# A decoder kernel with a new order in its first stage, gate and up projections apart in the experts, and one swap in the last stage

## The chip, the cores and the metric

One core of one Trainium2 chip runs the whole program in one launch. The metric is device time in microseconds (us), from three runs of the kernel before and as many of the kernel after. Engines are called PE (TensorE, the matmuls), PEld (its weight loads), DVE (VectorE), ACT (ScalarE), POOL (GpSimd) and SP (which only issues DMAs here).

## The reference

Two decoder layers on x of 8 x 256 tokens x 512 features, in float32, each sublayer followed by a layer norm of the sum. What matters here:

```python
# layer 0: differential attention, 16 pairs of heads of width 16 (4 shared key pairs), causal
q, k, v = x @ Wq.T, x @ Wk.T, x @ Wv.T
probs = softmax(mask(q k^T / 4)); o = probs @ v
attn = o[even heads] - lambda_full * o[odd heads]
attn = attn * rsqrt(mean(attn**2) + 1e-5) * ln_w * (1 - LAMBDA_INIT)
x = layernorm(x + attn @ Wo.T)
# layer 0: long convolution over pairs of channels with the context, plus a skip term; layernorm
# layer 0: 8 experts, the 2 best of each token
y = (silu(h @ gate.T) * (h @ up.T)) @ down.T      # gate, up: 512 -> 352; down: 352 -> 512
# layer 1: causal attention of 16 heads; attention over context and new tokens;
# layer 1: attention with keys and values picked from one of 16 heads by a gate
idx = argmax(x @ W_gate.T); k_shared = k[head idx]; v_shared = v[head idx] * top gate value
```

## The kernel before, in words

The program is a row of stages with a barrier between them: front (layer 0 attention and the sums of the skip term), conv (long convolution), middle (norms, routing), experts, tail (all of layer 1). In each stage every engine runs its own list of instructions in order; semaphores tie them together. No planner is in it: the order in the source is the order on the engine.

**Front.** One batch of 256 tokens passes through four phases, one a round, so that in round r the batches d = r, a = r-1, f = r-2 and u = r-3 are worked on together (`rounds()`). There are 11 rounds with work (r = 0 to 10); d ends after r = 7, a after r = 8, f after r = 9. On PE, batch d is transposed (`turn`) and projected (`query` x4, `value`, `key`). Batch a gets six score tiles (`score`, four banks of PSUM each), from which DVE takes the row maxima (`maxima`). All six share one tile of PSUM (`quads` has a single entry), so score n+1 waits for maxima n. Then `split_top` and `shift` bring the maxima to PE, six transposed score tiles (`scoreT`) follow, ACT takes their exponentials (`exps`), POOL masks (`causal`), and `weigh` multiplies with values ("O") and with ones ("Z"). ACT copies Z (`take_sums`), DVE builds the difference of heads (`combine`), ACT squares it, POOL adds epsilon (`add_eps`), PE sums over a head (`square_sums`), ACT takes the root (`root`), and DVE inverts it and scales (`scale_heads`, 128x512 each for ab = 0 and 1). `out` is the output projection, then `residual`, `statistics`, `norm`. Batch u is transposed once more (`turn("x1")`) and its skip term made (`skip_products` on DVE, `octets` on PE, `add_skip` on DVE). The other four banks of PSUM form a ring (`ring`): each use claims the next bank and waits until the use four claims earlier is drained, so the order on PE also decides who waits for whose reader.

**Experts.** 39 tiles of 128 token slots. For each tile PE gathers, transposes x (`turn_x`), computes gate and up (`gate_up`), transposes the product (`turn_hid`) and projects down (`down`); ACT takes silu and copies the transposed product (`hT`), DVE copies the transposed x and multiplies. The PE order is `gate_up(s+1)`, `turn_hid(s)`, `turn_x(s+2)`, `down(s)`.

**Tail.** Rounds again, with four phases P, C, H and A. In phase H the router of the shared keys (`gates`, 16 columns wide) and the keys and values of all heads (`rows("H", ...)`) are computed; DVE chooses the head (`gate_choice`) and picks (`pick`); ACT's exponential of the gate stands ahead of its copy of P's maxima (`take_shift("P")`).

## Time and profile before

| | us |
|---|---|
| median of 3 runs | 2350.17 (2348.56 to 2355.81) |
| the profiled execution, its own time | 2346.89 |
| its span, first to last instruction | 2345.2 |
| stretch of the front stage (to the first matmul of conv) | 0 to 569.7 |
| conv and middle | 569.7 to 989.8 |
| experts | 989.8 to about 1345 |
| tail | to 2345.2 |
| PE busy in the whole span | 2138.6 (91%) |
| mean granted clock of PE | 0.961 |

A row of a timeline gives the start, the duration, the engine, the line of the kernel, the operation, what it writes and reads, its shape, how many instructions were merged, and in brackets how long the engine had been idle before it and who ended that.

### The profile page before, as it was taken

Reading aid. Unit: us, or ns where it says so; the run is one execution under the profiler, and the core shown is the slowest. Engines: PE = TensorE matmul, PEld = TensorE weight load, DVE = VectorE, ACT = ScalarE, POOL = GpSimd, SP = SyncE. Lnnn points to the kernel's source line nnn. Section 1 sums busy time; section 2 is a strip of 40 time slices with the busy share of each in tenths; the row PEclk is TensorE's granted clock in tenths of the full one; section 3 lists DMA queues with packets and bytes.
Section 4 is the critical chain, followed back from the end, with each engine's and each line's share of the span. In section 5 each row is a group of like instructions: output and inputs, shape, how many; then the busy total and the mean of one; then the engine's idle time right before and its main releaser. Section 6 shows DMA issues by size and latency. Waiting matters only on the chain. (4 is left out here: it accounts for less than half of the span.)

```text
span 2345.2 us, 29072 instructions
## 1 busy us (share of the span) xinstructions
PE 2138.6 (91%) x11864; PEld 1233.3 (53%) x11872; DVE 1201.3 (51%) x1844; ACT 517.4 (22%) x783; POOL 574.9 (25%) x544
## 2 busy tenths in 40 slices
PE   6888898876999999799999888899999999999996
PEld 4434444422444466455555555566666665666553
DVE  2456666555989852022222223546656575747455
ACT  1444444431000021101111021222222222222121
POOL 1111111113777613211110221111322221211112
PEclk9999999997999999899999999999999999999997
DMA  9830000003211145921111250000010101000000
GB/s 173 96 33 28 28 28 19 30 10 123 93 40 45 34 142 131 212 73 63 63 60 58 89 203 28 28 18 28 19 37 18 43 13 37 1 28 10 1 10 19
DMA packets 66761, 129.62 MB, mean 55 GB/s; under 512 B 7450, under 2 KB 20968, under 8 KB 66632
## 3 DMA queue, kind: packets, MB, share of 16 engines
q1 hardware_dynamic: 44952, 75.43, 12.7%
q10 hardware_dynamic: 14976, 33.69, 5.3%
q0 software_dynamic: 6704, 18.64, 2.8%
q8 instruction: 98, 1.61, 0.3%
q14 instruction: 31, 0.25, 0.0%
HBM read 96.38 MB, written 41.85 MB: 59 GB/s over the span
## 5 line engine op out<-in xcount | busy, mean ns | idle before, releaser
L867 PE MATMUL conv_conv<-kv,toep 128*128 128x512 f32 x576 | 249.6, 596 | 4.6 <-POOL kv L888 4.6
L2157 DVE RECIPROCAL tail_inv<-tail_ring 128x256 f32<-128x256 f32 x64 | 112.4, 1757 | 181.8 <-PE tail_ring L1625 181.6
L1340 PE MATMUL moe_gu_ps<-gu,moe_xT 128*128 x624 | 193.1, 463 | 2.2 <-DVE moe_xT L1405 2.2
L867 PEld LDWEIGHTS conv_conv<-kv,toep 128*128 128x128 f32 x576 | 110.2, 191 | 144.0 <-issue 136.3
L888 POOL TENSOR_TENSOR kv<-vT,cT 128x512 f32<-128x512 f32 x128 | 146.2, 1163 | 61.2 <-PE conv_conv L867 52.6
L1340 PEld LDWEIGHTS moe_gu_ps<-gu,moe_xT 128*128 128x128 f32 x624 | 119.2, 191 | 79.5 <-issue 22.2
L1902 POOL TENSOR_TENSOR tail_rstd_x<-tail_rstd_x,const_minus_half 128x2 f32<-128x2 f32 x32 | 22.6, 707 | 486.2 <-DVE tail_rstd_x L2109 486.2
L1909 POOL TENSOR_SCALAR_AFFINE_SELECT tail_expT<-tail_expT 128x1024 f32<-128x1024 f32 x64 | 70.5, 1101 | 290.7 <-ACT tail_expT L1979 289.8
L513 POOL TENSOR_SCALAR_AFFINE_SELECT front_expT<-front_expT 128x2048 f32<-128x2048 f32 x32 | 64.1, 2005 | 271.6 <-ACT front_expT L571 271.6
L1358 PE MATMUL moe_y_ps<-down,moe_hT 128*128 (+1 forms) x234 | 110.7, 609 | 12.5 <-ACT moe_hT L1394 12.5
L1409 DVE TENSOR_TENSOR moe_hid<-moe_gu_ps,moe_silu 128x352 f32<-128x352 f32 x39 | 20.5, 525 | 181.2 <-ACT moe_silu L1379 181.2
L1979 ACT ACTIVATE tail_expT<-tail_scores 128x1536 f32<-128x1536 f32 x64 | 92.8, 1450 | 80.8 <-PE tail_scores L1603 80.8
L571 ACT ACTIVATE front_expT<-front_scores 128x2048 f32<-128x2048 f32 x48 | 90.1, 1878 | 77.0 <-PE front_scores L352 77.0
L1316 POOL DMA_INDIRECT xg<-x_after,tokens x37 | 34.9, 945 | 286.7 <-PE moe_xT_ps L1330 286.7
L649 DVE TENSOR_REDUCE front_negtop<-front_scores 128x8 f32<-128x2048 f32 x32 | 73.2, 2287 | 55.0 <-PE front_scores L318 55.0
L2143 DVE TENSOR_TENSOR tail_allowed<-tail_scores,const_mask_bf 128x1024 f32<-128x1024 f32 x48 | 58.5, 1219 | 65.1 <-PE tail_scores L1578 64.5
L912 DVE TENSOR_REDUCE vT<-prod 128x64 f32<-128x512 f32 x128 | 87.8, 686 | 4.4
L1379 ACT ACTIVATE moe_silu<-moe_gu_ps 128x352 f32<-128x352 f32 x39 | 18.1, 463 | 300.4 <-PE moe_gu_ps L1340 300.4
L1912 POOL TENSOR_TENSOR tail_expT<-tail_expT 128x512 f32<-128x512 f32 x64 | 81.3, 1270 | 5.3
L1422 DVE COPY moe_y<-moe_y_ps 128x512 f32<-128x512 f32 x39 | 27.0, 692 | 90.6 <-PE moe_y_ps L1358 90.6
L1358 PEld LDWEIGHTS moe_y_ps<-down,moe_hT 128*128 128x128 f32 (+1 forms) x234 | 41.3, 190 | 58.9 <-issue 58.9
L178 PE MATMUL front_ring<-front_xT,front_wq 128*128 128x256 f32 x256 | 62.1, 392 | 11.1 <-ACT front_xT L546 11.1
(334 smaller groups left out, 3997.4 us busy)
## 6 DMA issues: line engine op xcount, KB each, us to landing
toep<-toeplitz SPq DMA_DIRECT2D x32, 320.0 KB, 2.9
y_slots<-moe_y ACTq DMA_DIRECT2D x39, 256.0 KB, 2.0
gu<-in_L_ffn_gate_up_proj SPq DMA_DIRECT2D x5, 1408.0 KB, 10.4
toeplitz<-filt_rows SPq DMA_DIRECT2D x1, 6144.0 KB, 66.0
front_e<-in_ctx SPq DMA_DIRECT2D x8, 512.0 KB, 4.5
toeplitz<-filt_rows SPq DMA_DIRECT2D x2, 2048.0 KB, 87.0
x_after<-x SPq DMA_DIRECT2D x8, 512.0 KB, 5.0
tail_x<-x_after SPq DMA_DIRECT2D x8, 512.0 KB, 3.8
```

The lines of the kernel that those rows point to most:

```text
L513: pool.affine_select(out=tile, in_=tile, compare_op=ALU.is_ge, fill=0.0, base=0, pattern=[[0, 16], [1, P]], channel_multiplier=-1).then_in ...
L571: act.activation(exp_buf(b, n)[:].rearrange("p g j q -> p g (j q)"), scores[:], ACT.Exp).then_inc(quads.drained_sem(key), 1)
L649: ins = dve.tensor_reduce(negtop[:, 1, n].rearrange("p (g a) -> p g a", a=2), scores[:].rearrange("p g (a k) -> p g a k", a=2), AX_X, ALU. ...
L867: ins = pe.matmul(bank, toep[p][:, mat * P:(mat + 1) * P], kv[p][:, c].rearrange("p b j i -> p (b j i)"), start=n == 0, stop=n == len(PART ...
L888: pool.tensor_tensor(kv[p][:, c], tokens_of(c, h), context_of(c, h, 3), ALU.mult).then_inc(kv_ready, 1)
L912: dve.tensor_reduce(vT[:, lc, :, h * NI:(h + 1) * NI], prod[lc % 2][:], AX_X, ALU.add)
L1340: ins = pe.matmul(gu_ps[:, s % 2, h, 0:HID], xT[:, c, :], wgu[c][:, e, h * HID:(h + 1) * HID], start=c == 0, stop=c == NC - 1)
L1358: ins = pe.matmul(y_ps[:, s % 2, :], hT[0:w, n, :], wd[n][0:w, e, :], start=n == 0, stop=n == 2)
L1909: pool.affine_select(out=diagonal, in_=diagonal, compare_op=ALU.is_ge, fill=0.0, base=0, pattern=[[0, 8], [1, P]], channel_multiplier=-1). ...
L1912: pool.tensor_tensor(e[:, 3], e[:, 0], e[:, 2], ALU.add).then_inc(masked[kind], 1)
L1979: act.activation(exp_buf(kind, b, c)[:, 0:3].rearrange("p n g q -> p g n q"), scores[:, :, 0:3 * P].rearrange("p g (n q) -> p g n q", q=P) ...
L2157: link.after(dve.reciprocal(inv[c % 2][:], bank[:, S:2 * S]))
```

## The change

Three places change. **Front:** the order on PE, ACT and DVE is written anew. Round 0 computes value and key first, on a wait for their two weights alone (the query weights have a semaphore of their own), and the queries after. In the rounds with a batch a, the transposes of u move behind score 3, the octets move between scoreT 0 and 1, and `out(f, 0)` behind scoreT 1. On DVE the reciprocal of `scale_heads` is cut in halves of 128x256 (`invert`), and for ab = 0 these stand behind maxima 0 and maxima 3, with the scaling behind maxima 4; the skip products move behind maxima 1, and `residual(f, 0)` behind `add_skip`. The round with a = 7 has an order of its own (reciprocals after the maxima, `weigh` and `out` exchanged), and so have the two closing rounds, where `out(7, t)` waits for its own half of the scaling only. **Experts:** `gate_up` is cut into `gate` and `up`, with `turn_hid` between them; silu waits for the gate alone. **Tail:** the keys' first rows are computed ahead of the gates.

```diff
                 def out(b, t):
-                    pe.wait_ge(mixed, 2 * b + 2)
+                    pe.wait_ge(mixed, 2 * b + 2 + (t if b == B - 1 else 0))
...
+
                 pe.wait_ge(constants_made, 7)
                 for r, d, a, f, u in rounds():
-                    if a is not None: score(a, 0)
-                    if f is not None: square_sums(f, 0)
-                    if d is not None:
-                        if d == 0:
-                            pe.wait_ge(weights_loaded, 16 * len(MATS))
-                            pe.wait_ge(wq_grouped, 2)
-                        for n in range(2):
-                            drained(("turn", d, n))
-                        query(d, 0)
-                    if a is not None: score(a, 1)
-                    if f is not None: weigh(f, 1, 1, ("O",))
-                    if u is not None:
-                        pe.wait_ge(normed, u + 1)
-                        turn("x1", u, x[u % NX])
-                    if a is not None: score(a, 2)
-                    if f is not None:
-                        weigh(f, 1, 1, ("Z",))
-                        pe.wait_ge(e_loaded[f % NE], 16 * (f // NE) + 16)
-                        turn("ctx", f, e[f % NE])
-                    if a is not None: score(a, 3)
-                    if d is not None: value(d)
-                    if a is not None: score(a, 4)
-                    if d is not None: key(d)
-                    if f is not None: square_sums(f, 1)
-                    if a is not None: score(a, 5)
-                    if d is not None:
-                        query(d, 1)
-                        query(d, 2)
-                    if a is not None: shift(a)
-                    if d is not None: query(d, 3)
-                    if a is not None:
+                    if d == 0:
+                        xT_taken(d)
+                        pe.wait_ge(weights_loaded, 32)
+                        value(d)
+                        key(d)
+                        pe.wait_ge(wq_grouped, 2)
+                        for j in range(4):
+                            query(d, j)
+                    elif a is not None:
+                        score(a, 0)
+                        if f is not None: square_sums(f, 0)
+                        if d is not None:
+                            xT_taken(d)
+                            query(d, 0)
+                        score(a, 1)
+                        if f is not None: weigh(f, 1, 1, ("O",))
+                        score(a, 2)
+                        if f is not None:
+                            weigh(f, 1, 1, ("Z",))
+                            turn_context(f)
+                        score(a, 3)
+                        if d is not None: value(d)
+                        if u is not None: turn_tokens(u)
+                        score(a, 4)
+                        if d is not None: key(d)
+                        if f is not None: square_sums(f, 1)
+                        score(a, 5)
+                        if d is not None:
+                            query(d, 1)
+                            query(d, 2)
+                        shift(a)
+                        if d is not None: query(d, 3)
                         if a == 0:
...
                         scoreT(a, 0)
-                    if f is not None:
+                        if u is not None: octets(u)
+                        scoreT(a, 1)
                         if f == 0:
                             pe.wait_ge(wo_loaded, 64)
-                        out(f, 0)
-                    if a is not None: scoreT(a, 1)
-                    if u is not None: octets(u)
-                    if a is not None:
+                        if f is not None and a < B - 1: out(f, 0)
+                        if a == B - 1: weigh(a, 0, 0)
                         scoreT(a, 2)
-                        weigh(a, 0, 0)
+                        if a == B - 1: out(f, 0)
+                        else: weigh(a, 0, 0)
                         scoreT(a, 3)
-                    if f is not None: out(f, 1)
-                    if a is not None:
+                        if f is not None and a < B - 1: out(f, 1)
+                        if a == B - 1: weigh(a, 0, 1)
                         scoreT(a, 4)
-                        weigh(a, 0, 1)
+                        if a == B - 1: out(f, 1)
+                        else: weigh(a, 0, 1)
                         scoreT(a, 5)
                         weigh(a, 1, 0)
+                    elif f is not None:
+                        turn_tokens(u)
+                        turn_context(f)
+                        weigh(f, 1, 1)
+                        square_sums(f, 0)
+                        square_sums(f, 1)
+                        octets(u)
+                        for t in range(NT):
+                            out(f, t)
+                    elif u is not None:
+                        turn_tokens(u)
+                        octets(u)
...
-                act.dma_start(wq_rows, w["wq"].rearrange("(c p) e -> p c e", p=P)).then_inc(weights_loaded, 16)
+                act.dma_start(wq_rows, w["wq"].rearrange("(c p) e -> p c e", p=P)).then_inc(wq_loaded, 16)
...
-                act.wait_ge(weights_loaded, 16 * len(MATS))
+                for n in range(2):
+                    take(("turn", 0, n), pair(xT, n))
+                take_value(0)
+                act.wait_ge(half_made, 6)
+                take_key(0)
+                act.wait_ge(wq_loaded, 16)
...
                 for r, d, a, f, u in rounds():
-                    if d is not None:
+                    if d is not None and d:
                         for n in range(2):
                             take(("turn", d, n), pair(xT, n))
+                    if a is None and u is not None:
+                        for n in range(2):
+                            take(("x1", u, n), vT[:, 2 * n:2 * n + 2, u, :])
+                    if a is None and f is not None:
+                        for n in range(2):
+                            take(("ctx", f, n), cT[:, f, 2 * n:2 * n + 2, :])
+                        take_sums(f, 1, 1)
                     if f is not None: root(f, 0)
                     if d is not None: take_query(d, 0)
-                    if u is not None:
+                    if f is not None:
+                        if a is not None:
+                            take_sums(f, 1, 1)
+                            for n in range(2):
+                                take(("ctx", f, n), cT[:, f, 2 * n:2 * n + 2, :])
+                        squares(f, 1)
+                    if d is not None and d:
+                        take_value(d)
+                    if a is not None and u is not None:
                         for n in range(2):
                             take(("x1", u, n), vT[:, 2 * n:2 * n + 2, u, :])
-                    if f is not None:
-                        take_sums(f, 1, 1)
-                        for n in range(2):
-                            take(("ctx", f, n), cT[:, f, 2 * n:2 * n + 2, :])
-                        squares(f, 1)
-                    if d is not None:
-                        take_value(d)
-                        if d == 0:
-                            act.wait_ge(half_made, 6)
+                    if d is not None and d:
                         take_key(d)
                     if f is not None:
                         root(f, 1)
...
-                def scale_heads(b, ab):
+                def cols(t):
+                    return slice(t * P, (t + 1) * P)
+
+                def invert(b, ab, t):
                     key = ("sq", b, ab)
                     dve.wait_ge(ring.drained_sem(key), ring.count(key))
                     if b or ab:
                         dve.wait_ge(mixed, 2 * b + ab)
-                    link.after(dve.reciprocal(rinv[:], square[:, ab]))
+                    link.after(dve.reciprocal(rinv[:, :, cols(t)], square[:, ab, :, cols(t)]))
+
+                def scale_heads(b, ab):
                     dve.scalar_tensor_tensor(out=am[b % 2][:, ab], in0=am[b % 2][:, ab], scalar=lnw[:, 0:1], in1=rinv[:],
+                                             op0=ALU.mult, op1=ALU.mult).then_inc(mixed, 1)
+
+                def scale_half(b, ab, t):
+                    rows = am[b % 2][:, ab, :, cols(t)]
+                    dve.scalar_tensor_tensor(out=rows, in0=rows, scalar=lnw[:, 0:1], in1=rinv[:, :, cols(t)],
                                              op0=ALU.mult, op1=ALU.mult).then_inc(mixed, 1)
...
-                dve.wait_ge(weights_loaded, 16 * len(MATS))
+                dve.wait_ge(wq_loaded, 16)
...
                 for r, d, a, f, u in rounds():
+                    early = f is not None and a is not None and a < B - 1
                     if a is not None: maxima(a, 0)
+                    if early: invert(f, 0, 0)
+                    if a is not None: maxima(a, 1)
                     if u is not None: skip_products(u)
-                    if f is not None: scale_heads(f, 0)
+                    if a is not None: maxima(a, 2)
+                    if f is not None: combine(f, 1, 1)
+                    if a is not None: maxima(a, 3)
+                    if early: invert(f, 0, 1)
+                    if a is not None: maxima(a, 4)
+                    if early: scale_heads(f, 0)
                     if a is not None:
-                        maxima(a, 1)
-                        maxima(a, 2)
-                    if f is not None: combine(f, 1, 1)
-                    if a is not None:
-                        maxima(a, 3)
-                        maxima(a, 4)
                         maxima(a, 5)
                         split_top(a)
                     if f is not None:
-                        scale_heads(f, 1)
-                        residual(f, 0)
+                        if not early:
+                            for t in range(NT):
+                                invert(f, 0, t)
+                            scale_heads(f, 0)
+                        for t in range(NT):
+                            invert(f, 1, t)
+                            if a is None: scale_half(f, 1, t)
+                        if a is not None: scale_heads(f, 1)
                     if u is not None: add_skip(u)
+                    if f is not None: residual(f, 0)
                     if a is not None: combine(a, 0, 0)
                     if f is not None:
                         residual(f, 1)
...
-                def gate_up(s):
-                    e = expert(s)
+                def project(s, h, e):
+                    for c in range(NC):
+                        ins = pe.matmul(gu_ps[:, s % 2, h, 0:HID], xT[:, c, :], wgu[c][:, e, h * HID:(h + 1) * HID],
+                                        start=c == 0, stop=c == NC - 1)
+                    return ins
+
+                def gate(s):
                     pe.wait_ge(sem["xT_taken"], s + 1)
                     if s >= 2:
                         pe.wait_ge(sem["hid_ready"], s - 1)
-                    for h in range(2):
-                        for c in range(NC):
-                            ins = pe.matmul(gu_ps[:, s % 2, h, 0:HID], xT[:, c, :], wgu[c][:, e, h * HID:(h + 1) * HID],
-                                            start=c == 0, stop=c == NC - 1)
-                    ins.then_inc(sem["gu_ready"], 1)
+                    project(s, 0, expert(s)).then_inc(sem["gate_ready"], 1)
+
+                def up(s):
+                    project(s, 1, expert(s)).then_inc(sem["up_ready"], 1)
...
                 for s in range(TILES):
                     if s + 1 == HALVES[1][0]:
                         pe.wait_ge(mid.second_half, 16 * 6)
                     if s + 1 < TILES:
-                        gate_up(s + 1)
+                        gate(s + 1)
                     turn_hid(s)
+                    if s + 1 < TILES:
+                        up(s + 1)
                     if s + 2 < TILES:
                         turn_x(s + 2)
                     down(s)
...
-                    act.wait_ge(sem["gu_ready"], s + 1)
+                    act.wait_ge(sem["gate_ready"], s + 1)
...
                 def product(s):
                     dve.wait_ge(sem["silu_ready"], s + 1)
+                    dve.wait_ge(sem["up_ready"], s + 1)
                     dve.tensor_tensor(hid[:, s % 2, :], gu_ps[:, s % 2, 1, 0:HID], silu[:, s % 2, :], ALU.mult).then_inc(sem["hid_ready"], 1)
...
-                    if H_: turned("H", h); gates(h); rows("H", "k", h, 0, xT[h % 2], wide["gk"])
+                    if H_: turned("H", h); rows("H", "k", h, 0, xT[h % 2], wide["gk"]); gates(h)
```

## Rows read from the trace of the kernel before

**Rows 1.** The windows view, front stage and experts (busy us by engine, granted clock).
```profile
0.00:569.70 569.70, 464.64 (x2936) 221.50 (x2944) 307.01 (x367) 215.02 (x275) 103.26 (x95) 0.93 0.27 47
...
989.80:1345.00 355.20, 337.30 (x1163) 200.36 (x1164) 72.15 (x119) 35.82 (x119) 42.25 (x49) 0.99 0.22 72
```

**Rows 2.** The waits view, PE in the front stage: total, times, longest us.
```profile
PE front_scores L314 <- DVE front_negtop L649: 24.9, 11, 2.8
PE front_ring L378 <- POOL front_square L519: 15.1, 9, 3.6
PE front_ring L287 <- DVE front_cross L676: 12.0, 7, 1.7
```

**Rows 3.** The timeline of PE in one full round (r = 5).
```profile
271.06 1.09 PE L287 MATMUL front_ring<-const_ident,kept_wa 128*128 128x128 f32 x8
...
279.05 1.92 PE L371 MATMUL front_ring<-front_expT,front_v 128*32 128x512 f32 x16
...
284.82 1.03 PE L314 MATMUL front_scores<-const_mask_bf,const_ident_bf 128*128 128x256 bf16 x4 [2.82 <-DVE front_negtop L649]
...
287.80 3.34 PE L371 MATMUL front_ring<-front_expT,front_ones 128*32 128x512 f32 x16
292.87 1.06 PE L287 MATMUL front_ring<-const_ident,front_e 128*128 128x128 f32 x8 [1.72 <-DVE front_cross L676]
...
308.18 0.61 PE L337 MATMUL front_ring<-const_ident_bf,front_split 128*128 128x128 bf16 x8
```

**Rows 4.** The timeline of DVE in the same round.
```profile
277.11 1.40 DVE L694 SCALAR_TENSOR_TENSOR front_skipped<-kept_wvo,front_skips,front_e 128x512 f32<-128x512 f32 x2
278.44 3.34 DVE L687 RECIPROCAL front_rinv<-front_square 128x512 f32<-128x512 f32 x1
281.81 0.75 DVE L688 SCALAR_TENSOR_TENSOR front_am<-front_am,front_lnw,front_rinv 128x512 f32<-128x512 f32 x1
282.48 2.28 DVE L649 TENSOR_REDUCE front_negtop<-front_scores 128x8 f32<-128x2048 f32 x1
```

**Rows 5.** One line of the tail, by its durations: min/median/max ns.
```profile
L2157 DVE RECIPROCAL tail_inv<-tail_ring x64: 1748/1758/1759, 1407.9 to 2331.7; 128x256 f32<-128x256 f32 x64
```

**Rows 6.** The windows view: round 1 in part, rounds 4 and 5; the clock follows POOL.
```profile
35.00:80.00 45.00, 33.03 (x203) 17.24 (x202) 15.71 (x14) 11.81 (x14) 4.01 (x2) 0.81 1.01 101
209.00:270.00 61.00, 54.44 (x363) 26.57 (x364) 37.21 (x43) 25.51 (x35) 11.38 (x7) 0.97 0.08 27
271.00:333.00 62.00, 55.44 (x359) 26.63 (x360) 36.84 (x42) 25.09 (x35) 11.38 (x7) 0.94 0.08 26
```

**Rows 7.** The timeline of ACT and PE at the start.
```profile
14.25 1.05 ACT L593 COPY front_wq<-front_expT 128x1024 f32<-128x1024 f32 x1 [9.28 <-DMA front_wv<-in_L_attn_Wv]
...
18.97 3.75 PE L178 MATMUL front_ring<-front_xT,front_wq 128*128 128x256 f32 x8 [11.14 <-ACT front_xT L546]
...
32.15 1.04 PE L287 MATMUL front_ring<-const_ident,kept_wa 128*128 128x128 f32 x8
```

**Rows 8.** The timeline of PE in rounds 8 to 10 and at conv's start.
```profile
459.60 1.14 PE L318 MATMUL front_scores<-front_kT,front_qT 32*128 32x512 f32 x8
...
494.25 0.61 PE L349 MATMUL front_scores<-front_shiftT,front_pick 32*128 32x512 bf16 x4 [0.80 <-ACT front_shiftT L546]
...
519.49 1.04 PE L371 MATMUL front_ring<-front_expT,front_ones 128*32 128x512 f32 x8
...
545.49 5.98 PE L385 MATMUL front_ring<-front_wo,front_am 128*128 128x512 f32 x8 [4.86 <-DVE front_am L688]
...
569.74 5.80 PE L867 MATMUL conv_conv<-kv,toep 128*128 128x512 f32 x8 [4.57 <-POOL kv L888]
```

**Rows 9.** The waits view, PE in the experts.
```profile
PE moe_y_ps L1358 <- ACT moe_hT L1394: 12.5, 39, 0.7
```

**Rows 10.** The timeline of PE in one tile of the experts.
```profile
1107.43 0.60 PE L1330 MATMUL moe_xT_ps<-const_ident,xg 128*128 128x128 f32 x4
1108.33 2.84 PE L1358 MATMUL moe_y_ps<-down,moe_hT 128*128 x6 [0.30 <-ACT moe_hT L1394]
```

**Rows 11.** The timeline of DVE in phase H of the tail.
```profile
1684.92 0.75 DVE L2195 SCALAR_TENSOR_TENSOR tail_allowed<-tail_ring,tail_gval,tail_ind 128x512 f32<-128x512 f32 x1 [1.19 <-PE tail_ring L185]
```

15 lines of the change are left out of this document (13 added, 2 removed).

## The prediction

> **What bounds the kernel now.** I read the windows by stage first: PE is busy 464.6 of 569.7 us in the front stage and 337.3 of 355.2 us in the experts [rows 1]. In both no other engine comes near, so PE's list sets the end, and an edit is worth the PE idle time that it takes away, plus what PE loses at its lower clock. The waits view then names the idle time of the front: 24.9 us for the row maxima in eleven waits, 15.1 us for the squares, 12.0 us for a bank that `combine` drains [rows 2]. The timelines of one round on PE and on DVE show why.
>
> In round 5 score 2 starts at 284.82 after 2.82 us of idling [rows 3]. It waits for maxima 1, which DVE starts only at 282.48, because the skip products (1.40), the whole reciprocal (3.34) and the scaling (0.75) stand before it [rows 4]. After that gap the clock is down: the same 16 weighing matmuls take 3.34 us where they took 1.92 a little earlier [rows 3]. Then the context's transposes wait 1.72 us for the bank of O [rows 3]. A fact to keep for the sums: a maxima is 2.28 us [rows 4], a score tile about 1.67 us, counted as the 1.14 of its float32 part [rows 8] and about half a us for its mask.
>
> **Full rounds (3 to 7).** I lay the new lists over the old durations, from the end of maxima 0. DVE: maxima 0 ends at 277.11. The half reciprocal has no row in the front; the bounds are half of 3.34, which is 1.67 [rows 4], and the 128x256 row of the tail, 1.76 [rows 5]. I take 1.76, the same shape. It ends at 278.9, while score 1 ends at 279.1, so it is hidden under score 1; if it grew by over 0.2 us, its excess would be on the path. Maxima 1 then runs to 281.5 and score 2 starts at 281.5, against 284.82: 3.3 us gained, and the idling left is 0.55 us (O ends at 280.97). The skip products (1.40) hide under score 2. PE goes on with Z (1.86) and the context's transposes. In the ring these now stand four claims behind `sq` and query 0, both long drained, so the 1.72 us wait goes. `value` inherits it: its bank is that of O. `combine` starts when maxima 2 (283.3 to 285.6) and ACT's copy of Z (285.8) are done and drains O about 0.85 us later, at 286.7; `value` comes at 287.5, after score 3. Margin 0.8 us. Score 4 waited 0.66 us for maxima 3; the transposes of u (0.93) now stand there, and the wait goes. The second half reciprocal (1.76) lies under score 4 (1.8), the scaling (0.75) under score 5. Sum: score 5 is over at 297.0, two queries (3.56) later `shift` stands at 300.55, where the last maxima and the split have ended at 299.9. Before, `shift` was at 308.18 [rows 3]: 7.6 us earlier in round 5.
>
> Of that, 2.8 us is the clock (the excess of five rows over their usual durations) and 4.8 us idle time. After `shift` nothing is gained: the octets (2.0) cover the exponentials between scoreT 0 and 1 as `out` did, and `out` covers those between 1 and 2. On DVE the halves for ab = 1 follow the split (2 x 1.76 + 0.75 = 4.3, to 304.2); `out(f, 0)`, which waits for them, now comes at about 307.8, so the cut there costs nothing (0.17 us, being 2 x 1.76 less 3.34, hidden by 3.6 us). The 1.1 us wait at the head of each round stays: it is the chain combine, square, epsilon, and nothing in it is changed.
>
> Five such rounds give 5 x 4.8 = 24 us. For the clock, the mean granted clock is 0.97 in round 4 and 0.94 in round 5 [rows 6], so 61 us x 0.03 = 1.8 and 62 x 0.06 = 3.7 us were lost; the other three stand like round 4. That is 11 us at most; by the single rows it is 8.8. The new rounds have gaps of 1.1 and 0.55 us only, where I see no fall in these rows, so I count 8.5. Bounds: 0 and 11.
>
> **Round 2** has no u. The same wait goes there, smaller without the skip products, and its clock had not fallen: 2 us. Rounds 0 and 1: see next.
>
> **Start.** ACT now takes the transposes of batch 0 at about 8 us instead of 17.8, and PE can begin when the value weights land, 14.2 us by the wait of ACT's copy [rows 7]. But ACT's copy of the query weights (1.05 us) now stands behind `take_value` and `take_key`, and these wait for PE. Value and key are 16 and 8 matmuls, 4.7 us as before and up to 6.6 at the low clock in which PE starts after a pause (the first 8 matmuls took 3.75 us, twice the usual 1.9) [rows 7]. So they end at about 20.8; `take_key` (0.84) and the copy end at 22.8; four queries (7.2, up to 9 at the low clock) end at 30.0 to 31.8, against 32.15 [rows 7]. I take 1.5 us, bounds 0 and 3. Round 1 has the same list as before: 0.
>
> **Rounds 8 to 10.** Score 0 ends at 460.7 and scoreT 0 starts at 494.25 [rows 8]. It is a chain of score and maxima (4.1 us a link with its signals) with too much between. With the reciprocals behind the split (8.5 us, needed only by `out(6, 0)` some 10 us later) the chain is six links after DVE is free at 462.6, and reaches scoreT 0 at about 489: 5.3 us. `weigh(7, 0, 0)` directly behind scoreT 1 then waits 0.85 us for POOL, but the two waits of `out` go. Round 8 ends about 6 us earlier, from 520.5 [rows 8]. In round 9 PE starts with the transposes instead of 3.6 us of waiting for the squares, though these wait about 1.9 us for `norm` and O another 1.9 for ACT, which is still in its squares: 1.5 us gained. The octets fill the wait before `out(7, 0)` (1.9), which waits for half a reciprocal and half a scaling less (1.6 + 0.3), and part of its 5.98 us at the low clock comes back [rows 8] (1): 4.8 us. From the last `out` to conv, 13.1 us, nothing changes. Sum 6 + 1.5 + 4.8 = 12.3, taken as 12; bounds 6 and 16, since these are chains of signals with the least cover.
>
> **Experts.** Each tile ends `turn_x` and then idles 0.30 us until ACT has copied the transposed product; 12.5 us over 39 tiles [rows 9]. With `up` (half of 4.7 us) between `turn_hid` and `turn_x`, the copy (0.73 us with its start) is long done. Between the start of `turn_x` and that of `down` lie 0.90 us [rows 10]; four transposes alone take 0.53 to 0.59 elsewhere, so 0.31 to 0.37 may go. Against it stands one more seam, transposes then a wide matmul, whose first weight load of 0.19 us is longer than the 0.11 between transposes: 0.05 to 0.08. I take 0.30 x 38 = 11.4, as 11.5; bounds 0.23 x 38 = 9 and 0.37 x 38 = 14. `up` reads its expert number from memory once more; `down` has such a read at the same kind of place, behind four transposes, and the whole gap there is 0.30 us [rows 10], so at the worst it gives all back: lower bound 0. DVE's product now waits for `up` and has the rest of the tile.
>
> The Trainium skill, on the page TensorE: Matmul & The Clock Gate (Architectural detail), says that PE's queue is 64 deep and can pull weight loads ahead of matmuls in flight. By that rule the new seam costs nothing and the experts would give 14 us, the whole sum 62 instead of 59.5. The trace shows weight loads started before the matmul ahead of them has ended, but no seam of this kind in this stage.
>
> **Tail.** The same PE work in another order. The gates come 3.5 us later, and DVE's choice and key pick (1.4 + 2.1) then end at about 1685.05, where the value pick had waited 1.19 us for PE until 1684.92 [rows 11]. ACT's gate exponential ends about 0.6 us after the maxima arrive, with over 2 us until scoreT needs them. So 0; bounds -3 and +2 over six rounds.
>
> **Sum.** 24 + 8.5 + 2 + 1.5 + 12 + 11.5 + 0 = 59.5 us. Against the profiled execution's own 2346.9 that is 2287.4; this execution lies 3.3 us below the median of the runs, so against 2350.2 it is 2290.7.
>
> **Rivals.** *B, the front gives about half* (a fifth of the chance): a margin of 0.2 to 0.8 us is overrun in each full round, `value` or score 2 is late, and the clock falls as before. For it: every margin is thin, and DVE rows are longer where POOL runs. Then 24 + 8.5 becomes about 8, the ends 7: 59.5 - 24.5 - 5 = 30, at 2320. *C, the experts give nothing*, because the second read of the expert number costs the 0.3 us: 2302. Against it: the read stands behind no unmet wait and can run ahead. *D, slower: PE's clock.* In round 1, where short gaps alternate with scores, the mean clock is 0.81 [rows 6], so 0.19 of the stretch is lost. If seven rounds of 54 us ran like that, it would cost 72 us less the 11 lost already, 61 more, and my gain without the 8.5 is 51: 2360. It decides from a mean clock of about 0.84 on. Against it: those gaps were 2.4 us each, the new ones half of it or less. *E, nothing changes*: the gain is eaten by waits that I don't see, such as `combine` in `value`'s way by 7 us a round; the margins speak against it.
>
> **How the numbers follow.** Forecast 0.64, B 0.17, C 0.09, D 0.05, E 0.05. The likeliest own range is 2280 to 2302 (clock 0 to 11, ends 6 to 16, start 0 to 3, experts 9 to 14 do not all fail together). 2275 to 2320 leaves out D, E and the further half of B. A measurement of this kernel tells 0.3%, or 7 us, from no change. Faster 0.90 (forecast, B, C), same 0.05 (E), slower 0.05 (D).
>
> **What would show it.** Right: full rounds of 54 us instead of 61 or 62, no wait over 1.2 us on PE in them, a clock of 1.00; conv's first matmul at about 522; no wait of `down` and 8.3 to 8.4 us a tile instead of 8.64; the tail as long as before. Wrong: a new wait of `value` or score 4, a half reciprocal of over 2 us, low clock in the full rounds, or a gap ahead of `up`.

## The result, and the profile after

The changed kernel takes 2278.38 us (median of four, 2275.38 to 2281.46) against 2350.9 us before (four runs too): ratio 0.9698, 95% interval 0.9673 to 0.9724. That is 72.5 us, where 59.5 was forecast (2290.7). It lies inside the whole range, 3 us above its lower end of 2275, and just outside the likeliest one (2280 to 2302). The profiled execution took 2275.38 us, its span is 2273.6, its clock 0.966.

Cut at the first matmul of each stage, the two profiles give the table below. In the profile before these cuts lie at 569.7, 987.9 and 1334.9 us; the 989.8 and "about 1345" of the section on the time before were cut more roughly.

| stage | before, us | after, us | gained | forecast |
|---|---|---|---|---|
| front | 569.7 | 523.7 | 46.0 | 48 |
| conv and middle | 418.2 | 419.0 | -0.8 | 0 |
| experts | 347.0 | 326.9 | 20.1 | 11.5 |
| tail | 1010.3 | 1004.1 | 6.2 | 0 |

The windows view, front (its last figures are busy us by engine, clock, DMA) and two full rounds (answers to [rows 1, 6]):

```profile
0.00:523.70 523.70, 455.11 (x2936) 220.99 (x2945) 315.22 (x384) 215.22 (x275) 103.64 (x95) 0.95 0.30 52
...
210.00:265.00 55.00, 52.97 (x367) 26.25 (x368) 39.09 (x47) 26.55 (x34) 11.38 (x7) 1.00 0.09 30
266.00:321.00 55.00, 52.97 (x363) 26.25 (x365) 39.19 (x47) 26.55 (x34) 11.38 (x7) 1.00 0.09 30
```

The waits view, PE in the front (answers to [rows 2]):

```profile
PE front_ring L379 <- POOL front_square L546: 12.3, 8, 4.0
PE front_scores L315 <- DVE front_negtop L688: 10.8, 11, 2.4
...
PE front_ring L178 <- ACT front_wq L625: 1.9, 1, 1.9
...
PE front_ring L372 <- DVE front_cross L715: 1.1, 1, 1.1
```

Ahead of the scores of this form the maxima held PE 24.9 us and now 10.8. The bank that `combine` drains held the transposes 12.0 us; now it holds one weighing with the ones, for 1.1. The squares' wait was to stay and is 1.1 us in each full round. The timeline of PE in round 5 (answers to [rows 3]) shows how:

```profile
261.71 1.92 PE L372 MATMUL front_ring<-front_expT,front_v 128*32 128x512 f32 x16
264.27 0.61 PE L315 MATMUL front_scores<-const_mask_bf,const_ident_bf 128*128 128x256 bf16 x4 [0.63 <-DVE front_negtop L688]
...
265.88 1.92 PE L372 MATMUL front_ring<-front_expT,front_ones 128*32 128x512 f32 x16
267.73 1.09 PE L288 MATMUL front_ring<-const_ident,front_e 128*128 128x128 f32 x8
...
272.15 1.04 PE L288 MATMUL front_ring<-const_ident,kept_wvo 128*128 128x128 f32 x8
...
283.34 0.61 PE L338 MATMUL front_ring<-const_ident_bf,front_split 128*128 128x128 bf16 x8
```

and DVE beside it (answers to [rows 4]):

```profile
257.57 2.28 DVE L688 TENSOR_REDUCE front_negtop<-front_scores 128x8 f32<-128x2048 f32 x1
259.77 1.74 DVE L729 RECIPROCAL front_rinv<-front_square 128x256 f32<-128x256 f32 x1
261.92 2.29 DVE L688 TENSOR_REDUCE front_negtop<-front_scores 128x8 f32<-128x2048 f32 x1 [0.41 <-PE front_scores L319]
```

Score 2 waits 0.63 us (forecast 0.55), the matmuls with the ones take 1.92 us where they took 3.34, and the context's transposes wait for nobody. DVE idles 0.41 us ahead of maxima 1: the half reciprocal (1.74; forecast 1.76) is hidden with that much to spare. From the head of round 5 to `shift` are 29.6 us (253.72 to 283.34) where they were 37.1: 7.5 us less, 7.6 forecast.

### The profile page after: what moved, and what is told of

Same layout as the page of the kernel before. It is cut to its first block and busy times, and to the rows that moved or that the text cites. A ratio compares the mean times of both kernels' runs of the same rounds, so it can differ in the third digit from the quotient of the medians.

```text
span 2273.6 us, 29273 instructions
## 1 busy us (share of the span) xinstructions
PE 2116.7 (93%) x11864; PEld 1231.1 (54%) x11872; DVE 1231.6 (54%) x1861; ACT 517.4 (23%) x783; POOL 589.0 (26%) x544
## 3 DMA queue, kind: packets, MB, share of 16 engines
q1 hardware_dynamic: 44952, 75.43, 13.1%
q8 instruction: 99, 1.62, 0.3%
## 5 line engine op out<-in xcount | busy, mean ns | idle before, releaser
L1393 PE MATMUL moe_gu_ps<-gu,moe_xT 128*128 x624 | 199.6, 463 | 3.4 <-issue 1.8
L946 POOL TENSOR_TENSOR kv<-vT,cT 128x512 f32<-128x512 f32 x128 | 160.5, 1275 | 48.7 <-PE conv_conv L925 38.9
L1968 POOL TENSOR_TENSOR tail_rstd_x<-tail_rstd_x,const_minus_half 128x2 f32<-128x2 f32 x32 | 22.6, 707 | 482.1 <-DVE tail_rstd_x L2175 482.1
L985 DVE TENSOR_TENSOR prod<-total,cT 128x512 f32<-128x512 f32 x64 | 74.8, 1168 | 2.2
L963 ACT COPY both<-conv_conv 128x512 f32<-128x512 f32 x32 | 18.7, 585 | 233.9 <-PE conv_conv L925 218.3
```

The lines of the kernel that those rows point to most:

```text
L946: pool.tensor_tensor(kv[p][:, c], tokens_of(c, h), context_of(c, h, 3), ALU.mult).then_inc(kv_ready, 1)
L1393: ins = pe.matmul(gu_ps[:, s % 2, h, 0:HID], xT[:, c, :], wgu[c][:, e, h * HID:(h + 1) * HID], start=c == 0, stop=c == NC - 1)
```

## The experiments

Medians compare only inside a group, where all ran on one chip with the kernel before: first group e1, e2, e3, e5; second e4, e6, e7, e8; third e9 to e12. Before takes 2361 to 2363 us there. The changed kernel itself ran in the third group only (e9), so where e4 to e8 are set beside it, it is by their ratios to before, and a difference of 0.2% (the changed kernel gave 0.9698 and 0.9715) says nothing. "Front" is the time of conv's first matmul in a kernel's profile; all such stretches are from one execution each, and one program's front differs by up to 3 us from profile to profile, with PE's clock (see "Rounds 9 and 10").

### One part alone: e1, e2, e3

e1 is the kernel before with the new front, e2 with the new experts, e3 with the swap in the tail.

```diff
 e1: -front_stage of before    +front_stage of after
 e2: -experts_stage of before  +experts_stage of after
 e3: -gates(h); rows("H", "k", h, 0, ...)   +rows("H", "k", h, 0, ...); gates(h)
```

> The kernel before with the new front stage alone. Theory (parts are local): conv's first matmul moves from 569.7 to about 524, a gain of 46 us, and experts and tail keep their lengths (341 and 1010 us). Rival (parts act on each other through PE's clock): the tail shortens by several us here too, though nothing in it is changed, and the gain is 50 us or more.

> The kernel before with gate and up apart, and nothing else. Theory (from the rows after): a tile takes 8.09 us instead of 8.64, 38 tiles give 21 us. Rival (as predicted: only the 0.30 us wait goes and a seam costs): 11.5 us, and the other 10 us seen in this stage are of another cause.

> The kernel before with the keys' first rows ahead of the gates in the tail, and nothing else. Theory (the order): low-clock stretches behind the gates in rounds 4 and 5 of the tail vanish, a gain of 5 to 6 us, and the key rows take 3.67 us in all rounds. Rival (where PE's clock falls in the tail depends on what came before, not on this order): low stretches at other places, a gain of 0 to 2 us.

Before 2362.97. e1 2315.21, ratio 0.9803 (0.9785 to 0.9822); e2 2342.59, 0.9925 (0.9907 to 0.9942); e3 2354.38, 0.9967 (0.9953 to 0.9981). The parts sum to 1.97 + 0.75 + 0.33 = 3.05%; the whole gave 3.02% and, in e9, 2.85%, each with about 0.25 either way: they add within that, and nothing shows that one lives on another. In e1 the front ends at 525.2 us and the tail keeps its 1010.3, so the rival of e1 is out. e3 alone is 8 us (4 to 11 by its interval, 7.0 in its tail), where I had put the tail's swap at nothing; e2 is 18 us (14 to 22; its experts take 327.9 us, 19.1 less than before), where I had 11.5.

### The changed kernel once more: e9

No edit. It is the control for the third group, and shows what two profiles of one program differ by.

> The changed kernel once more, unaltered, beside its variants on one chip. In the runs so far conv and middle took 13 to 20 us longer than in the first profile of either kernel, whatever the kernel. Theory: this goes with the chip, so it shows here too (432 to 439 us), and the ratio to before stays at 0.970. Rival: it belongs to something in the variants; then conv and middle are back at 419 us here.

2294.71 (2290.06 to 2303.66) against 2362.78, 0.9715 (0.9691 to 0.9739). Front 523.2, experts 327.8, tail 1004.7: as in the profile after. Conv and middle take 437.2 us instead of 419.0: the unaltered kernel shows it too, so it does not come from the variants, as its theory had it (more below).

### The full rounds: e4 and e5

e4 takes the reciprocal of ab = 0 whole, behind maxima 0. e5 puts the transposes of u back between the weighing of O and score 2 (and ACT's copy of them ahead of that of the sums).

```diff
 e4:
-                    if early: invert(f, 0, 0)
+                    if early: invert_whole(f, 0)     # 128x512
...
-                    if early: invert(f, 0, 1)
 e5:
                         if f is not None: weigh(f, 1, 1, ("O",))
+                        if u is not None: turn_tokens(u)
                         score(a, 2)
...
                         if d is not None: value(d)
-                        if u is not None: turn_tokens(u)
```

> The changed kernel with the reciprocal for ab = 0 in one piece (128x512) behind maxima 0, the scaling still behind maxima 4. Theory: 3.34 us stand where 1.9 are free, so score 2 starts 1.6 us later in rounds 2 to 7, 10 us if the clock holds; the gap before score 2 grows from 0.6 to 2.2 us. Rival 1: the clock falls behind this gap as it did before, another 1.4 to 2.8 us in five rounds, 17 to 20 us in all. Rival 2: the halves did nothing, since the place of the scaling alone made room: 0 to 3 us.

> The changed kernel with the transposes of u back between the weighing of O and score 2, on PE and ACT; the DVE order stays new. Theory (the bank matters): the context's transposes wait for O's bank again, 1.5 us, score 4 waits 0.66 us for maxima 3 again, and score 2 starts 0.4 us later: 2.3 to 2.6 us in each of rounds 3 to 7 and in round 8, 12 to 15 us slower than the changed kernel (gain 58 to 60 instead of 72). Rival (only DVE's order mattered, the place of the transposes fills idle time anyway): under 4 us, gain 68 or more.

e4: 2303.52 against 2361.13, 0.9759 (0.9742 to 0.9775), against 0.9715 for e9. Front 535.7, 12.5 us more than e9's; 3.6 of that are in round 1, which the edit does not touch, and rounds 2 to 7 are 9.4 us longer. Its PE timeline in rounds 4 and 5:

```profile
216.24 0.61 PE L315 MATMUL front_scores<-const_mask_bf,const_ident_bf 128*128 128x256 bf16 x4 [1.86 <-DVE front_negtop L688]
216.78 1.60 PE L319 MATMUL front_scores<-front_kT,front_qT 32*128 32x512 f32 x8
218.31 3.10 PE L372 MATMUL front_ring<-front_expT,front_ones 128*32 128x512 f32 x16
...
275.00 0.61 PE L315 MATMUL front_scores<-const_mask_bf,const_ident_bf 128*128 128x256 bf16 x4 [1.86 <-DVE front_negtop L688]
275.54 1.14 PE L319 MATMUL front_scores<-front_kT,front_qT 32*128 32x512 f32 x8
276.61 1.92 PE L372 MATMUL front_ring<-front_expT,front_ones 128*32 128x512 f32 x16
```

Score 2 waits 1.86 us instead of 0.63 in all six rounds from 2 to 7, that is 7.4 us. In rounds 4 and 6 the clock fell after it (the weighing takes 3.10 and 3.27 us), and score 2 is followed by the context's transposes after 5.1 us instead of 3.5, 3.3 us in all; in rounds 2, 3, 5 and 7 it stayed up (1.92). The granted clock of rounds 4 and 6 is 0.97, of the others 1.00. So both terms hang on this wait: behind 2.82 us of idling the clock was down [rows 3], behind 1.86 in two rounds of six, behind 0.63 in none. The theory's 10 us are met, but with a smaller wait than its 2.2 and a part of its first rival.

e5: 2306.16 against 2362.97, 0.9766 (0.9747 to 0.9784). Front 534.8, 11 us more. Its PE timeline in the same round:

```profile
274.56 1.06 PE L288 MATMUL front_ring<-const_ident,front_e 128*128 128x128 f32 x8 [1.71 <-DVE front_cross L715]
...
279.77 0.81 PE L323 MATMUL front_scores<-const_mask_bf,const_ident_bf 128*128 128x512 bf16 x3 [0.66 <-DVE front_negtop L688]
```

Both waits of before are back, 1.71 and 0.66 us (1.72 and 0.66 before), 2.4 us a round. Score 2 in turn waits for nothing, so a round pays 1.71 + 0.66 - 0.63 = 1.74 us: rounds 3 to 7 take 57.6 us instead of 55.9, 8.6 us in five. In round 8 the bank's wait is 1.71 too and score 4 waits 2.64 us instead of 1.62; `shift` stands 32.8 us after the first score instead of 29.4. That is less than the 2.3 to 2.6 us a round of the theory, which let score 2 start later on top of both waits. The clock is 1.00 in its rounds 3 to 7: the gap of 1.71 us in this place did not lower it. The claims on the ring, and work ahead of score 4, are the mechanism.

### The experts: e6 and e7

e6 keeps the order of before and lets silu start after the gate. e7 puts `turn_hid` ahead of both products, so that ACT's copy is again early, but `gate` and `up` stand together.

```diff
 e6:
                         gate(s + 1)
+                        up(s + 1)
                     turn_hid(s)
-                    if s + 1 < TILES:
-                        up(s + 1)
 e7 (ACT copies hT ahead of silu):
+                    turn_hid(s)
                     if s + 1 < TILES:
                         gate(s + 1)
-                    turn_hid(s)
-                    if s + 1 < TILES:
                         up(s + 1)
```

> The changed kernel, but gate and up follow each other again on PE before the transposes of the product; silu still waits for the gate alone. Theory (the gain is the wait for ACT's copy and the weight loads held up by it): the 0.30 us wait before down is back, a tile takes 8.64 us, 21 us slower than the changed kernel. Rival (the early silu gives part of it, ACT's queue being free for the copy): the wait is shorter, 8.3 us a tile, 10 us slower.

> The changed kernel, but the product is transposed ahead of gate and up, which then follow each other; ACT copies it before its silu. Theory (any place that hides the copy does, and a seam costs nothing that can be seen): 8.08 us a tile, the same time as the changed kernel within 2 us. Rival 1 (each seam between transposes and wide matmuls costs 0.05 to 0.08 us): the same number of seams on one side but one switch less, 2 to 3 us faster. Rival 2 (the product of tile s is late, since silu and product follow up(s) by 1 us and the down projection gives them 2.6 us): a new wait ahead of the transposes, slower.

e6: 2311.04, 0.9792 (0.9776 to 0.9809); experts 347.0 us, exactly that of before, with 11.5 us of waits for `hT` in 39 places and 8.61 us a tile. Early silu alone gives 0.03 us a tile, and the 8.3 of the rival is out. e7: 2291.11, 0.9707 (0.9691 to 0.9724); experts 325.9, 1 us less than after, with the same 8.08 us a tile. What counts is that some product stands between `turn_hid` and `down`; one more or one less seam is not seen.

### The start: e8 and e10

e8 moves ACT's copy of the query weights ahead of its takes of value and key; e10 is e8 and e7 together.

```diff
+                act.wait_ge(wq_loaded, 16)
+                act.copy(...wide["wq"]..., ...wq_rows...).then_inc(wq_grouped, 1)
                 take_value(0)
                 act.wait_ge(half_made, 6)
                 take_key(0)
-                act.wait_ge(wq_loaded, 16)
-                act.copy(...wide["wq"]..., ...wq_rows...).then_inc(wq_grouped, 1)
```

> The changed kernel with ACT's copy of the query weights ahead of its reads of value and key in round 0. Theory (the query weights land at about 8.6 us, well before the value weights at 14.3): the 1.93 us gap before the first queries goes and the whole is 2 us faster (gain 74 to 75). Rival (the clock: PE's queries then run earlier, at the low clock): 0 to 1 us.

> The changed kernel with both variants that looked no worse: ACT's copy of the query weights first, and the product transposed ahead of gate and up. Theory (local gains add): 2 to 3 us from the start and 1 us from the experts, 3 to 4 us faster than the changed kernel. Rival: both are below what can be told, 0.

e8: 2292.64, 0.9715 (0.9699 to 0.9732), the ratio of e9: the 2 us that the theory names are not seen in the medians. The timeline of after and then of e8:

```profile
14.63 3.67 PE L185 MATMUL front_ring<-front_wv,front_xT 128*128 128x128 f32 x16 [6.82 <-DMA front_wv<-in_L_attn_Wv]
18.14 1.89 PE L178 MATMUL front_ring<-front_xT,front_wk 128*128 128x256 f32 x8
21.96 7.17 PE L178 MATMUL front_ring<-front_xT,front_wq 128*128 128x256 f32 x32 [1.93 <-ACT front_wq L625]
28.97 1.04 PE L288 MATMUL front_ring<-const_ident,kept_wa 128*128 128x128 f32 x8
```

```profile
18.07 2.62 PE L178 MATMUL front_ring<-front_xT,front_wk 128*128 128x256 f32 x8
20.53 7.07 PE L178 MATMUL front_ring<-front_xT,front_wq 128*128 128x256 f32 x32
27.43 1.04 PE L288 MATMUL front_ring<-const_ident,kept_wa 128*128 128x128 f32 x8
```

The gap of 1.93 us is gone, and round 0 ends 1.5 us earlier than in the profile after, 4.4 earlier than in e9's. Key took 2.62 us here and 1.89 in the profile after, so part of the gap is given back, as the rival says. The copy had its data from 8.5 us on and stood in the queue behind work that waits for PE. e10: 2289.63 against e9's 2294.71 in the same group; 0.9697 (0.9680 to 0.9713) against 0.9715 (0.9691 to 0.9739). It has the lowest median of its group, and the intervals overlap: a gain over the changed kernel is likely and not measured.

### The ends of the front: e11 and e12

e11 scales ab = 1 of the last batch whole, and both `out(7, t)` wait for that. e12 gives the round with a = 7 the order of all others.

```diff
 e11:
-                    pe.wait_ge(mixed, 2 * b + 2 + (t if b == B - 1 else 0))
+                    pe.wait_ge(mixed, 2 * b + 2)
...
-                            if a is None: scale_half(f, 1, t)
-                        if a is not None: scale_heads(f, 1)
+                        scale_heads(f, 1)
 e12:
-                    early = f is not None and a is not None and a < B - 1
+                    early = f is not None and a is not None
...
-                        if f is not None and a < B - 1: out(f, 0)
-                        if a == B - 1: weigh(a, 0, 0)
+                        if f is not None: out(f, 0)
                         scoreT(a, 2)
-                        if a == B - 1: out(f, 0)
-                        else: weigh(a, 0, 0)
+                        weigh(a, 0, 0)
```

(and the same for t = 1 in e12)

> The changed kernel with the last scaling of round 9 in one piece, both output projections waiting for it. Theory (out waits for DVE there): out(7,0) starts 1.7 to 1.9 us later. Rival (the octets at the low clock end when the half scaling does, so out waited for PE, not for DVE): under 1 us.

> The changed kernel with round 8 in the order of the full rounds: reciprocals between the maxima, out(6,0) behind scoreT 1. Theory (the row by row estimate): the reciprocals fit into the gaps of the score chain (1.76 under 1.7), so the score half is as long, while the second half saves the 0.85 us wait of the weighing: 0 to 1 us faster. Rival (round 8's own order is what gave the 4.7 us): 3 to 5 us slower.

e11: 2291.82, 0.9702 (0.9683 to 0.9722). Its `out(7, 0)` waits 2.04 us for DVE and starts 79.7 us after round 8's first score, 77.6 in e9; conv starts 1.1 us later by the same count. That is the theory's size, half a reciprocal and half a scaling, partly given back, and too small for the medians. But in the profile after the halves gave nothing: there PE, slower before it, comes to `out(7, 0)` only 80.2 us after that score (421.71 to 501.86), later than in e11. The row in the profile after, in e9 and in e11:

```profile
501.86 7.49 PE L386 MATMUL front_ring<-front_wo,front_am 128*128 128x512 f32 x16
```

```profile
501.62 7.20 PE L386 MATMUL front_ring<-front_wo,front_am 128*128 128x512 f32 x16
```

```profile
503.39 7.13 PE L386 MATMUL front_ring<-front_wo,front_am 128*128 128x512 f32 x16 [2.04 <-DVE front_am L732]
```

e12: 2290.82, 0.9692 (0.9675 to 0.9709). The timeline of after, then of e12, where round 8 gives over to round 9:

```profile
455.01 3.65 PE L393 MATMUL front_ring<-front_skipped,const_octets 128*128 128x512 f32 x4
...
479.58 1.06 PE L372 MATMUL front_ring<-front_expT,front_ones 128*32 128x512 f32 x8 [1.08 <-DVE front_cross L715]
483.10 1.97 PE L288 MATMUL front_ring<-const_ident,kept_wa 128*128 128x128 f32 x8 [2.45 <-DVE kept_wa L776]
```

```profile
481.18 1.04 PE L372 MATMUL front_ring<-front_expT,front_ones 128*32 128x512 f32 x8
482.57 1.09 PE L288 MATMUL front_ring<-const_ident,kept_wa 128*128 128x128 f32 x8 [0.35 <-DVE kept_wa L772]
```

From round 8's first score to conv, e12 takes 95.7 us (424.54 to 520.20) and e9 99.2 (423.98 to 523.18): in these profiles the round's own order costs 3.5 us, where the theory had 0 to 1 and the rival the opposite sign. In the profile after the same stretch is 102.0 us, and in the six other profiles whose front ends like the changed kernel's (e1, e4, e6, e7, e8, e10) it is 99.2 to 101.9. Neither were e10 and e12 run together, nor was e12 taken often enough for the medians to say it.

## Why the prediction was right, step by step

**Full rounds: right.** From the start of the run to round 8's first score the kernel gained 37.4 us (459.07 to 421.71). Without the start (3.2) and round 2 (1.7) that leaves 32.5 for five rounds, the 24 + 8.5 of the sum. That the total is met to the tenth is luck: by PE's busy time in the five rounds (278.3 to 268.4 us) the clock gave 9.8 and the idle time 22.6, so the one was put 1.3 too low and the other 1.4 too high. A round is 55.9 us and not the "54" of the text: the full rounds of before take 61.4 to 63.4 us by their first scores, the "61 or 62" were the windows that I had read and not the rounds. The clock is 1.00 in rounds 4 and 5. e4 and e5 bring back the waits that the steps name, and no others. Rival B (a margin overrun) and rival D (the clock falls in shorter gaps) did not occur: no gap in a full round is over 1.1 us, and the clock is up behind each. By e4, D's condition was not far: 1.2 us more at one place, and the clock falls in two rounds of six.

**Start: under-sized.** 3.2 us (32.15 to 28.97) for 1.5. The order of events was as laid out: value from 14.63, the copy after `take_key`, 1.93 us of waiting. The four queries ran at full clock (7.17) and key too. In e9 they took 8.86 and round 0 ended at 31.84, with a granted clock of 0.80 in the queries where it was 1.00: the upper end that I named also happens. The nine profiles with this start end round 0 at 28.6 to 31.8 us, the three with the old one at 31.2 to 32.2, so what the start gives is about 0 to 3.5 us from run to run.

**Round 2:** 1.7 us for 2.

**Round 8: the step that failed.** 2.5 us for 6. The first half is as worked out: scoreT 0 comes 31.05 us after the first score, 35.18 before (4.1 for 5.3). The second half was to be 0.7 us shorter and got longer, 27.9 us for 26.3. The "two waits of `out`" that were to go have no row: the trace of before shows no wait ahead of either `out(6, t)`. Two things were not in my sum. The octets, now behind scoreT 0 and the gaps of the score chain, run at the low clock (3.65 us instead of 1.98; before, `out(6, 0)` stood there and lost 1.2), and the last weighing with the ones waits 1.08 us for the bank of O, which `combine` drains late because `residual(6, 1)` and `statistics(6)` stand ahead of it on DVE. After it the transposes wait 2.45 us for `norm` (1.9 was said). In e12, without the exchange, the first of these waits is gone and the second is 0.35 us.

**Rounds 9 and 10: right in this pair of profiles,** 6.1 us for 6.3, but partly by luck. From the end of round 8 to conv the profile after takes 43.1 us and e9, the same program, 40.3: which one meets 6.3 is the clock's doing (in the profile after the first weighing of round 9 takes 3.10 us and the second squares 2.08, in e9 1.92 and 1.12). By the stretch from round 8's first score to conv, after, e1, e7 and e10 take 101.8 to 102.0 us and e4, e6, e8 and e9 99.2. The wait ahead of `out(7, 0)`, 4.86 us before, is gone, but in the profile after not by the halves (e11): the octets run at the low clock (3.62 us) and end later than the scaling. And "from the last `out` to conv nothing changes" did not hold: 14.4 us for 13.1, since the last octets took 3.62 us for 2.37.

**Experts: mechanism right, mis-sized by almost half.** 20.1 us for 11.5. The wait went in every tile but one and rival C is out: a tile is 8.08 us, 8.64 before. The step that failed is the "0.31 to 0.37 may go", for which I took 0.30: I had subtracted the transposes' duration, but the next matmul starts before the row of the transposes has ended. PE and then its weight loads in one tile of after (answers to [rows 10]):

```profile
1062.29 0.49 PE L1411 MATMUL moe_hT_ps<-const_ident,moe_hid 128*128 128x128 f32 x3
1062.62 2.53 PE L1393 MATMUL moe_gu_ps<-gu,moe_xT 128*128 x8
1064.99 0.60 PE L1388 MATMUL moe_xT_ps<-const_ident,xg 128*128 128x128 f32 x4
1065.42 2.74 PE L1420 MATMUL moe_y_ps<-down,moe_hT 128*128 x6
```

```profile
1064.99 0.36 PEld L1388 LDWEIGHTS moe_xT_ps<-const_ident,xg 128*128 128x128 f32 x3 [0.15 <-issue]
1065.32 0.30 PEld L1420 LDWEIGHTS moe_y_ps<-down,moe_hT 128*128 128x128 f32 x2
```

and the loads of before at the same place:

```profile
1107.32 0.47 PEld L1330 LDWEIGHTS moe_xT_ps<-const_ident,xg 128*128 128x128 f32 x4
1108.32 0.30 PEld L1358 LDWEIGHTS moe_y_ps<-down,moe_hT 128*128 128x128 f32 x2 [0.53 <-issue]
```

`down` starts 0.43 us after `turn_x` instead of 0.90. Its weights are the copied product itself, so before the semaphore held their load back as well as the matmul: the load began at 1108.32, with the matmul. Now it begins ahead of it, at 1065.32, in the shadow of the transposes. So the 0.30 us in the waits view was the visible part of 0.47, and `down` is 0.1 shorter (2.74 for 2.84), since its first load is no longer inside it. The seam that I charged 0.05 to 0.08 for costs nothing: transposes to product is 0.33 us (1062.29 to 1062.62), which is what transposes to transposes took before (1107.10 to 1107.43). The Trainium skill (TensorE: Matmul & The Clock Gate, Architectural detail) has PE pull weight loads ahead of matmuls in flight; by that rule the seam was free and the stage worth 14 us. The trace agrees on the seam, and the measured gain is larger still.

**Tail: mis-sized, 0 forecast, 6.2 measured** (bounds -3 and +2; e3 confirms a gain). The static gain is 0.1 us a round. The rest is the clock, which I did not read there, though the two slow key rows stood in the trace of before. PE in round 4 of phase H, before and then after:

```profile
1786.87 0.66 PE L1681 MATMUL tail_ring<-const_ident,tail_mixedT 128*128 128x128 f32 x4 [0.45 <-ACT tail_probs L1985]
1787.88 2.40 PE L185 MATMUL tail_ring<-tail_wgate,tail_xT 128*128 128x16 f32 x16 [0.35 <-ACT tail_xT L1962]
1790.11 6.59 PE L185 MATMUL tail_ring<-tail_gk,tail_xT 128*128 128x512 f32 x8
```

```profile
1722.04 0.66 PE L1747 MATMUL tail_ring<-const_ident,tail_mixedT 128*128 128x128 f32 x4 [0.45 <-ACT tail_probs L2051]
1723.05 3.67 PE L185 MATMUL tail_ring<-tail_gk,tail_xT 128*128 128x512 f32 x8 [0.35 <-ACT tail_xT L2028]
1726.56 1.85 PE L185 MATMUL tail_ring<-tail_wgate,tail_xT 128*128 128x16 f32 x16
```

After the same two gaps (0.45 and 0.35 us) gates and keys took 9.0 us in one order and 5.5 in the other; the granted clock there was 0.69 (1786 to 1797 us) and 1.00 (1722 to 1729). With the gates first, the keys were slow in 2 of 6 such rounds in the profile of before (6.59 and 5.37 us for 3.68), in 2 of 6 in e1 (5.06, 6.49) and in 1 of 6 in e2 (5.12), 5 of 18; with the keys first, in none of 66 (after and e3 to e12). In the stage's last two rounds, where other work lies around them, the key rows are slow in either order (5.42 and 5.02 us before, 4.57 and 4.23 after). The two rounds of before lost 3.4 and 1.7 us by their length (115.55 and 113.87 us, the others 112.18); at the stage's two ends smaller gains and losses nearly cancel. The tail takes 1008.1 to 1010.3 us in the three profiles with the gates first and 1003.3 to 1004.7 with the keys first, but for e12: there it takes 1008.6, and what it has more lies in the stage's opening, ahead of the first gates. Why the clock falls behind the gates and not behind the keys was not tried by itself.

**The whole.** The misses are +1.7 (start), -3.5 (round 8), +8.6 (experts), +6.2 (tail): the two that I had under-sized most are both work whose duration I had kept fixed when its place changed. Three of the four lie on one side; the range held them because it was wide, not because the sizes were known.

## What to carry to other kernels

A wait of PE for the operand that it must load as weights can cost more than the waits view says (here 0.47 us for a shown 0.30), since it holds the load too: look at where the weight load starts and not only at the matmul's bracket. Of two orders with the same work, one can keep the clock and the other not (here the keys were slow in 5 of 18 rounds behind the gates, in 0 of 66 ahead of them): check each slow row against its usual duration before costing a swap at nothing. Where a round is a chain of signals, write down who drains each bank at the exchange: e12 suggests that the round which got an order of its own would have been better with the common one. And take the control twice before reading 1 us out of one profile: two profiles of this program differ by 2.8 us in the last three rounds of the front alone.

## What the runs showed of the hardware

**One stage differed between the groups of runs.** Conv and middle took 418.2 and 419.0 us in the first profiles of before and after, 431 to 432 in e2 and e3 and 435 to 439 in the ten later profiles with the new front, on three chips, one for each group. No run on the first pair's chip was repeated beside them, so that the chip is the cause is likely and not shown. The waits view of e9 there:

```profile
PE midl_ring L1105 <- issue: 7.2, 5, 2.9
PE midl_ring L1097 <- issue: 5.8, 5, 1.7
```

In the profile after these two rows do not appear. They lie 366 to 391 us after conv's start, with kernels of both fronts, and sum to 11.2 us (e3) to 16.0 us (e11). They lengthen before and after alike, but a few us between two profiles can come from them; I know no cause for them.

**A cost that stays open.** In ten of the eleven profiles with the new front the middle's first projections end 3.3 to 3.7 us later after conv's start than in the three with the old one (274.1 to 274.5 for 270.8 us), in a window at a lower clock (0.83 for 1.00). In e11, which has the new front too, they end at 271.0, with a clock of 1.00, so the new front does not bring this about every time. The stretch of conv and middle is longer by 4 to 7 us with the new front on the later chips (435 to 439 for 431 to 432), by 0.8 in the first pair; e11 is at 435.5, where the waits above are the longest, 16.0 us for e2's 12.1. This may be part of why e9's gain, 68 us, is below 72.5, though the two intervals overlap. No run tells whether something in the front leads to it.
